# The last FFN block's gate and up as two products with whole numbers, group by group

## The reference, cut to what matters

```
def dequantize(imatrix, scales, zeros, group_size, out_dtype):      # group_size 128
    rs = jnp.repeat(scales, group_size, axis=0)
    rz = jnp.repeat(zeros, group_size, axis=0)
    return ((imatrix - rz) * rs)
gate = silu(x @ gate_proj)         # x: 2048 x 512, gate_proj: 512 x 1792, 4 groups of 128 rows
up   = x @ up_proj                 # 512 x 1792
out  = (gate * up) @ down_proj     # 1792 x 512
x    = layernorm(x + out)
```

## Time and profile before

| What | Value |
|---|---|
| Median of three executions | 1409.56 us |
| Profiled execution, its own time | 1409.34 us |
| Its span | 1407.5 us |
| Mean granted TensorE clock | 0.981 |
| PE busy | 1330.7 us (95% of the span) |
| DVE busy | 1030.7 us (73%) |
| ACT busy | 795.1 us (56%) |
| POOL busy | 766.2 us (54%) |

### The profile page before, as it was taken

The page is one execution under the profiler, slowest core; times in us unless marked ns, Lnnn a source line. Parts: engine busy times, 40 slices in busy tenths (PEclk is TensorE's granted clock), DMA queues, the critical chain, the costliest instruction groups (busy, mean ns, idle before and its releaser), DMA issues. The chain is left out here.

```text
span 1407.5 us, 32864 instructions
## 1 busy us (share of the span) xinstructions
PE 1330.7 (95%) x11934; PEld 978.2 (69%) x11934; DVE 1030.7 (73%) x2328; ACT 795.1 (56%) x1753; POOL 766.2 (54%) x963
## 2 busy tenths in 40 slices
PE   5788999989999999999999899999999999999998
PEld 2445866677678777868686667667777768586775
DVE  6988887876778889877777787968696778665121
ACT  3877787877687868877885244333424432331221
POOL 3656688688787577887544435254434434351221
PEclk8879999999999999999999999999999999999999
DMA  7573578578985554787662100641001000000000
GB/s 207 160 177 83 124 136 165 134 136 154 166 162 131 119 127 113 146 179 140 137 129 48 46 1 16 256 135 38 8 9 38 16 1 34 20 9 16 1 16 16
DMA packets 232356, 131.95 MB, mean 94 GB/s; under 512 B 151738, under 2 KB 215458, under 8 KB 231298
## 3 DMA queue, kind: packets, MB, share of 16 engines
q1 hardware_dynamic: 230956, 129.77, 39.9%
q10 hardware_dynamic: 1238, 0.07, 0.1%
HBM read 75.00 MB, written 19.92 MB: 67 GB/s over the span
## 5 line engine op out<-in xcount | busy, mean ns | idle before, releaser
L2004 PE MATMUL ps<-x3h,w1gu 128*128 128x256 f16 x1792 | 298.9, 273 | 3.4 <-DVE prod L1657 3.4
L1255 ACT ACTIVATE Pe<-ps,nmax 128x256 f32<-128x256 f32 (+3 forms) x512 | 252.8, 535 | 62.2 <-DVE nmax L1398 36.2
L1398 DVE TENSOR_REDUCE nmax<-ps 128x1 f32<-128x384 f32 (+3 forms) x352 | 222.7, 635 | 42.3 <-PE ps L1894 37.9
L2004 PE MATMUL ps<-x3l,w1gu 128*128 128x256 f16 x896 | 244.2, 273 | 0.0
L2004 PEld LDWEIGHTS ps<-x3h,w1gu 128*128 128x128 f16 x1792 | 175.3, 98 | 28.1 <-DVE prod L1657 5.0
L1393 DVE TENSOR_TENSOR pt<-ps,pt 128x512 f16<-128x512 f32 (+1 forms) x256 | 161.3, 632 | 34.8 <-ACT pt L1239 33.8
L1135 POOL TENSOR_TENSOR int1l<-prod,int1h 128x256 f16<-128x256 f32 x112 | 95.5, 858 | 137.1 <-ACT int1h L1354 137.1
L1239 ACT ACTIVATE pt<-ps 128x512 f16<-128x512 f32 (+1 forms) x256 | 143.3, 560 | 39.4 <-PE ps L1901 30.4
L1891 PE MATMUL ps<-kT,qT 128*128 128x256 f16 (+3 forms) x512 | 138.2, 305 | 16.0 <-ACT Pe L1255 15.0
L1901 PE MATMUL ps<-identf,Pe 128*128 128x128 f32 x928 | 148.0, 279 | 2.9 <-DVE pt L1393 2.0
L838 POOL TENSOR_TENSOR stp<-Pe,stp 128x512 f16<-128x512 f32 (+1 forms) x96 | 103.9, 1082 | 40.6 <-ACT stp L1247 40.5
(11 more groups left out here) (269 smaller groups left out, 3377.6 us busy)
## 6 DMA issues: line engine op xcount, KB each, us to landing
w1gu<-w_gu SPq DMA_DIRECT2D x7, 1024.0 KB, 8.1
x_dram<-xr SPq DMA_DIRECT2D x18, 256.0 KB, 3.1
xr<-in_x SPq DMA_DIRECT2D x16, 256.0 KB, 3.5
x2a<-x_dram SPq DMA_DIRECT2D x4, 1024.0 KB, 5.7
vq<-in_q1g SPq DMA_DIRECT2D x28, 128.0 KB, 2.5
vz<-in_z1g SPq DMA_DIRECT2D x28, 128.0 KB, 3.9
vs<-in_s1g SPq DMA_DIRECT2D x28, 128.0 KB, 4.6
w_gu<-vh SPq DMA_DIRECT2D x56, 64.0 KB, 2.3
```

What stands on the lines that cost most here:

```text
L1255: ins = act.activation(Pe[:, u % 2, x * w:(x + 1) * w], ps[:, u % 2, x * w:(x + 1) * w], ACT.Exp, bias=nmax[:, u % 4, x:x + 1])
L1398: dve.tensor_reduce(nmax[:, u % 4, 0:g], ps[:, u % 2, 0:g * w].rearrange("p (g w) -> p g w", g=g), AX, ALU.max, negate=True).then_inc(sem( ...
L2004: ins = pe.matmul(ps[:, bank, piece * H2:piece * H2 + H2], w1gu[:, j // 2, 2 * piece + pw, k, cols], px[:, k, h * H2:h * H2 + H2], start=( ...
```

## The change

FFN blocks 0 to 2 are computed as before. In block 3, whose column tiles are m = 84 to 111, gate and up are each computed as four separate sums with the whole numbers q - z (times 256, exact in float16), one per row group: 2 matmuls (`x3h`, `x3l`) of 256 columns for each. Two groups share a PSUM bank, so step `f1_gq (m, x)` is 4 matmuls: x = 0 and 1 are gate's groups, x = 2 and 3 up's. ACT `q_a` reads the first group, scaled by a column of scales `scol`, into SBUF (`q_out`, in the space of `yc` and `xc`); DVE `q_d` adds the other three, each with its scale, by `scalar_tensor_tensor`. The banks are five that hydra no longer needs. `f1_down` of block 3 waits for each `f1_lo` by itself, and its pieces are placed among the `f1_gq` steps.

For this POOL `w1_q` writes its second result in float16 (`vi`), SP stores it as well, in place of one of the two stores of the halves, which are now one DMA; SP loads it over `w1gu` (`w1_whole`, seven DMAs) while block 2 still runs; ACT issues two DMAs for `scol`. The last `w1s` store now precedes `weights_a` on SP. Some semaphores are merged. The tables of the planner have other values, and `LO_POOL` no longer names tiles 3, 6 and 7: their 48 `p_lo` steps go from POOL to DVE.

```diff
-LO_POOL = (3, 6, 7, 12, 13, 14, 15)
+LO_POOL = (12, 13, 14, 15)
...
+Q_BANKS = (1, 3, 4, 2, 0)
...
             for j in range(NJ1):
                 m = gate1(f, h, j)
                 e = None
-                for piece in range(2):
+                for x in range(4 if f == LAST else 0):
+                    q = q_no(m, x)
+                    A("PE", "f1_gq", (m, x), 445, [("x3l", (f, 2 * h + 1)), ("w1_whole", j // 2), ("q_d", q_key(q - NQB)) if q >= NQB else ("x3l", (f, 3 if q == 4 else 2)) if q >= 3 else None], mm - 1)
+                    if x % 2 == 0:
+                        A("ACT", "q_a", (m, x), 400, [("f1_gq", (m, x)), ("f1_prod", m - 2) if m - 2 >= gate1(LAST, 0, 0) else ("x3l", (f, 1))], soon)
+                    A("DVE", "q_d", (m, x), 920 if x % 2 else 440, [("q_d", (m, x - 1)), ("f1_gq", (m, x))] if x % 2 else [("q_a", (m, x))], soon)
+                for piece in range(0 if f == LAST else 2):
...
-WO_AT = 0
-CH0_AT = [-10 + 0.5 * c for c in range(NC0)]
+WO_AT = 4
+CH0_AT = [-14 + 0.6 * c for c in range(NC0)]
 CH1_AT = [CH0_AT[-1] + 6 + 4 * c for c in range(NC1)]
-IN_AT = [-20, -10] + [FIRST[t] - 24 for t in range(2, NT)]
+IN_AT = [-20, -10, -6, 74, 67, 72, 64, 111, 83, 112, 173, 37, 134, 274, 270, 293]
...
+                if kind == "scol":
+                    act.wait_ge(sem("ld_x3_1"), 16)
+                    for n, k in enumerate("gu"):
+                        act.dma_start(scol[:, n, :, :], A[f"s1{k}"].rearrange("g (j p) -> p g j", p=P), allow_slow_non_contiguous=True).then_inc(sem("ld_tab_s1"), 16)
+                if kind == "q_a":
+                    m, x = key
+                    q = q_no(m, x)
+                    act.wait_ge(sem("f1_gu"), gate1(LAST, 0, 0) + q + 1)
+                    if q == 0:
+                        act.wait_ge(sem("ld_tab_s1"), 80)
+                    if q >= 8:
+                        act.wait_ge(sem("f1_prod"), m - 1)
+                    act.activation(q_out[m % 2][:, x, :], ps[:, Q_BANKS[q % NQB], 0:H2], ACT.Copy,
+                                   scale=scol[:, x // 2, 0, m % NJ1:m % NJ1 + 1]).then_inc(sem("q_a"), 1)
...
+            if kind == "q_d":
+                m, x = key
+                q = q_no(m, x)
+                to = q_out[m % 2][:, x - x % 2, :]
+                if x % 2:
+                    dve.wait_ge(sem("f1_gu"), gate1(LAST, 0, 0) + q + 1)
+                    dve.wait_ge(sem("q_d"), q)
+                    own.link(dve.scalar_tensor_tensor(out=to, in0=ps[:, Q_BANKS[q % NQB], 0:H2], scalar=scol[:, x // 2, 2, m % NJ1:m % NJ1 + 1], in1=to,
+                                                      op0=ALU.mult, op1=ALU.add))
+                else:
+                    dve.wait_ge(sem("q_a"), q // 2 + 1)
+                g = 1 + x % 2 * 2
+                dve.scalar_tensor_tensor(out=to, in0=ps[:, Q_BANKS[q % NQB], H2:S], scalar=scol[:, x // 2, g, m % NJ1:m % NJ1 + 1], in1=to,
+                                         op0=ALU.mult, op1=ALU.add).then_inc(sem("q_d"), 1)
+                return
...
+        def pe_groups(pe, m, x):
+            q, h, j = q_no(m, x), m // NJ1 % 2, m % NJ1
...
+            if q >= NQB:
+                pe.wait_ge(sem("q_d"), q - NQB + 1)
...
+            for n in range(2):
+                g = 2 * (x % 2) + n
+                for part, px in enumerate((x3h, x3l)):
+                    ins = pe.matmul(ps[:, Q_BANKS[q % NQB], n * H2:n * H2 + H2], w1gu[:, j // 2, x // 2 * 2, g, cols],
+                                    px[:, g, h * H2:h * H2 + H2], start=(part == 0), stop=(part == 1))
+            ins.then_inc(sem("f1_gu"), 1)
```

## The result

The changed kernel takes 1417.80 us (median of 6 runs, 1415.06 to 1419.49) against 1410.02 us of the kernel before, run beside it (6 runs, 1407.79 to 1413.32). The ratio is 1.0049, 95% interval 1.0033 to 1.0066: slower by 0.5%, some 6.9 us. The forecast was 1405 us. The profiled execution has a span of 1417.7 us, 10.2 more than the one of before; it is the slowest of the six.

The account below looks back on a forecast made before the run. The prediction took PE to bound the kernel before, and VectorE to become block 3's bound. Its terms, -6.0 (block 3), +6.0 (scol) and -4 (attention), sum to -4 us on 1409.3: 1405 us, range 1391 to 1421 us.

Parts of the forecast that it names:

- Block 3, -6.0: Block 3: PE's gate and up matmuls take 24.4 us less, but 18.4 of it is lost, netting -6.0 us.
- 3.31 us: Block 3: VectorE's predicted time for one column tile's seven instructions, against 1.75 us for PE's 16 matmuls.
- five steps are between an instruction and one that needs its result and carry the 0.06 (0.51 each): Block 3, VectorE: five dependent steps per tile at 0.45 us from an earlier pair plus 0.06 for the scale column.
- upper bound of 0.15 us per dependent step: Block 3: if all 140 dependent VectorE steps cost 0.15 us more, 21 us are added and the term becomes +15.
- Rival 3: Block 3: dependent VectorE steps cost no more than others, 14 us less, 1391 us; chance 0.08.
- scol, +6.0: Ahead of uh 3: issuing the two scol loads holds ACT 5.4 us, and PE's slower clock adds about 1; +6.0 us.
- Rival 1: Ahead of uh 3: the scol loads aren't felt, as the queue takes them or descriptors are cheaper; 1399 us, chance 0.20.
- rival 2: Ahead of uh 3: scol loads felt fully at 39 ns, ACT held 26 us, PE runs dry; 1426 us, chance 0.12.
- Order and p_lo, -4: Attention and first FFN: half of ACT's 23.9 us waiting for p_lo goes, about a third reaches PE; -4 us.
- Rival 4: Attention's first 300 us: VectorE becomes the bound, late nmax and ptl make +8 instead of -4; 1417 us, chance 0.15.
- Whole numbers and stores, nothing: Weight preparation: w1_q's float16 result and merged stores leave instruction counts as they are, so cost nothing.
- Rival 5: Block 3: PE's short waits make its clock fall and stay down, adding 49 us; some 1440 us, chance 0.05.

Follow-up runs that it names:

- e10: The changed kernel with a constant instead of the scol column in VectorE's six additions per tile of block 3; ratio to the kernel before 0.9966.
- e8: The changed kernel without VectorE's second waits in block 3 (before the odd q_d; f1_prod's for f1_hi), dependences kept; ratio to the kernel before 1.0012.
- e12: e8 with f1_prod's wait for f1_lo moved ahead of the tile's first q_d; ratio to the kernel before 0.9989.
- e4: The changed kernel with block 3's groups reordered so VectorE's additions alternate between gate's and up's sums; 1399.51 us, ratio to the kernel before 0.9932.
- e13: The kernel before with the changed kernel's tables, LO_POOL and three planner entries, without whole numbers or the new block 3; ratio to the kernel before 0.9974.
- e15: e13 with the 48 p_lo of tiles 3, 6 and 7 back on GpSimd; ratio to the kernel before 1.0015.
- e6: The kernel before, its planner untouched, with only the 48 p_lo of tiles 3, 6 and 7 moved to VectorE; ratio to the kernel before 1.0021.
- e14: e13 with the whole numbers prepared as in the changed kernel, but not used by block 3; ratio to the kernel before 0.9994.
- e3: The changed kernel with the two scol loads issued by SP instead of ACT; ratio to the kernel before 1.0014.
- e9: The changed kernel with output tile 15's f1_down pieces allowed between tile 14's as their f1_lo comes; ratio to the kernel before 0.9953.

## Why the prediction was wrong

The mechanism was right: block 3 turned from PE's to VectorE's bound, `scol` was felt, the order gave something. The sign came out wrong by sizes, and by a wait that had been put at nothing.

- **Block 3, -6.0: the step that failed.** Measured: +1.5 us by the marks, +2.8 +- 3 by the ratios. The step "3.31 us" per tile is 3.57. The 0.06 for a column is right (e10), and so is the step of a dependent pair with one wait (0.52 against my 0.51). What failed is "five steps are between an instruction and one that needs its result and carry the 0.06 (0.51 each)": I took all five for the pair of the earlier trace rows. In that pair the wait on the neighbour is the first; the odd `q_d` has one met wait ahead of it (+0.07, twice) and `f1_prod` three (+0.11), as e8 and e12 showed by taking them away. It is 0.26 us in each of 28 tiles, 7.3 us, less 0.8, since what is left between the tiles, the normalizations above all, is 9.2 us instead of 10.0. The end came out 1.3 us longer than 9.6 + 1.6, since PE waited 2.74 us and its matmuls behind that took twice their time at first. Behind the last matmul it is 0.3 us less. That is 7.3 - 0.8 + 1.3 - 0.3 = 7.5 us, the distance between forecast and trace. My upper bound of 0.15 us per dependent step held it, and the pace stayed just under the 3.6 us that I had named as the sign of a wrong size; I took the near row without comparing the waits in the code.
- **VectorE's order was open to choice.** The sum took the chain of six as a property of the scheme. e4 shows that it was the order in which they were written. Rival 3 (dependent steps cost no more than others) falls: 0.52 to 0.62 against 0.39. By the Trainium skill, VectorE: DVE Perf Modes, section The DRAIN you can't avoid, where a semaphore after each of eight copies costs nothing extra, they would be equal; the measurement decides.
- **scol, +6.0.** Measured 4.9 +- 3 by the ratios and 5.6 by the traces (4.46 - 0.43 = 4.0 us of idle time and 1.6 us of slower matmuls). Rival 1 and rival 2 fell. The mechanism holds, but that the size came near is in part luck. I had 224 rows per DMA engine taken at once and 672 to drain at 8.0 ns, 5.4 us. That 224 doesn't follow from the earlier trace rows, and the first load, with 448 rows per engine, was issued in 0.38 us. In the 4.42 us that ACT was held, 5742 packets moved, 359 per engine, and hardly any before 946.4 us, 1.2 us after the first issue; with 70.2% of the 16 engines' time taken, a packet kept its engine for 0.702 x 16 x 4.42 us / 5742 = 8.7 ns.
- **Order and p_lo, -4.** Measured -3.7 (-5.5 to -1.8), by e13. That the number fits is partly luck: the order without the move costs 2.1 us (e15), the move in it gains 5.8. The reason that I gave is only half true: the waits for `p_lo` halved as forecast, but those for `nmax` ate this wherever the order wasn't made for it (e6). And it was not a third of the waits that came out as time: the two sums above changed by +4.2 and -6.8 us, the time by +3.0 and -5.8. Rival 4 describes e6, not the change.
- **Whole numbers and stores, nothing.** Measured +2.8, the second step that failed. I named the counts of instructions as its cover and overlooked what they wait for: GpSimd's `w1_q` behind a store, 25.7 us of waits in e14. Whether the wait or the 3.7 MB of stores makes the 2.8 us stays open.
- **Rival 5** fell: the clock is 1.00 from 1290 to 1398 us with PE's waits at 0.7 us or less up to one of 1.57 us at its end, and it falls only behind the next, of 2.74 us.

The errors of the four terms are +8.8, -1.1, +0.3 and +2.8 us by the ratios, 10.8 in all; the forecast said -4, the ratio +6.9.

## What to carry to other kernels

When work moves from a full engine to an idle one, its price there is the distance from start to start, not the busy time: count the dependent steps and the waits ahead of each, and interleave two independent chains before deciding that the scheme doesn't pay (here 0.89 us of 3.57 per tile, and the difference between 0.5% slower and 0.7% faster). A load with short rows belongs on an engine for which nobody waits, since its issue holds the engine. Where a planner sets the order, a table and its costs are one edit: to measure a part, pin the order and move only the part.

## What the runs showed of the hardware that I had not expected

- A VectorE instruction of 256 columns that needs the one before it, with the wait on that one last in the row: 0.52 us from start to start with no other wait, 0.58 to 0.59 with one met wait ahead of it, 0.62 to 0.63 with two or three. With that wait first and two behind it the step is 0.45 us for an instruction of 0.42, no more than with one wait. An independent one follows after 0.39 to 0.40 us although each takes 0.48.
- A scale read from a column costs VectorE 0.06 us in each instruction of 256 columns, and it passes on whole to a dependent step (e10).
- Two loads with rows of 4 bytes, 7168 rows each, move one packet for each row, 14368 in all. The first is issued in 0.37 to 0.38 us and the second holds its engine for 4.40 to 4.42 us, on ACT's queue as on SP's.
- PE was idle for 3.57 us ahead of `in` and for 2.74 us ahead of the last `f1_down` pieces. Its granted clock was 0.50, the lower level, from 953.5 to 956 us and from 1400.6 to 1403.3 us, and 24 matmuls of `in` took 4.44 instead of 2.88 us, the first of `f1_down` 0.43 us each instead of 0.216. Without those waits (e3, e9) the clock is 1.00 in the same places.
